# A decoder layer's expert stage: features on the partitions, weights as the stationary operand

## The chip, the core and the metric

The kernel runs on one core of a Trainium2 chip. The metric is device time in microseconds. A core has TensorE (PE, matmuls into PSUM), VectorE (DVE), ScalarE (ACT), GpSimd (POOL) and SyncE (SP); each runs its own list of instructions in order, and semaphores tie the lists together.

## The reference

A decoder layer on x of 4 x 256 tokens with 128 features: self attention with fixed-point rounding, cross attention to 1601 context rows, and a mixture of 8 experts of which each token uses 2. All is f32. The part that the change touches:

```
gout = x @ Wgate + bgate ; top 2 of 8, softmax over the two weights
x1 = x @ W1[e] + b1[e]                  # 128 -> 256
x2 = x @ W2[e] + b2[e]
z  = x1 * x2
g  = z @ Wg[e] + bg[e]                  # 256 -> 256
o  = silu(g) * (z @ Wl[e] + bl[e])
y  = o @ W3[e] + b3[e]                  # 256 -> 128
out = x + sum over the two chosen experts of weight * y
```

## The kernel before

The layer is one program: projections and self attention (to about 270 us), cross attention (to about 605 us), then layer norm, routing and the expert stage. Routing sorts the 2048 (token, expert) pairs into blocks of 128 rows that belong to one expert each: at most NBLK = 23 blocks. The rows go through HBM (`xdisp`): POOL scatters them there, SP loads one block after the other into a ring of 6 (`xblk`), and POOL scatters the results to `ydisp` from a ring of 3 (`yblk`). At the end the two results of each token are loaded and added. Which expert a block has is read from `table` into a register of each engine that needs it (`value_load`), and the weights of all experts lie in SBUF: `w12` (W1 and W2 side by side, 512 columns an expert), `wgl` (Wg and Wl, 2 x 512), `w3_sb`.

One block before, with tokens on the partitions between the layers. Line numbers are those of the profile:

- `block_T` (L1205, TensorE) transposes the block's rows, `block_move` (L1448, ScalarE) copies them to SBUF.
- `up` (L1217): the transposed tokens are the stationary operand, 512 weight columns stream past; result 128 tokens x 512.
- `zed_of` (VectorE): adds the bias (L1817) from `bias_bc`, a copy of all biases on each of the 128 partitions, and multiplies the two halves (L1818).
- `zed_transposes` (L1225) and `zed_move` (L1454): the product, turned, for the next layer.
- `gate_linear` (L1233): two matmuls of 512 columns, accumulated.
- `gl_bias` (L1823), `gate_silu` (L1460), `ogl_of` (L1830).
- `ogl_transposes` (L1243) and `ogl_move` (L1466), `down` (L1251), `y_move` (L1473, which also scales by the routing weight), the scatter (L815).

The blocks are interleaved by hand. In iteration j TensorE's list has: up(j), ogl_transposes(j-2), block_T(j+1), gate_linear(j-1), the register load for j+1, zed_transposes(j), down(j-2). VectorE's has zed_of(j), gl_bias(j-1), ogl_of(j-1), and after the first zed_of the table of the later blocks. ScalarE's has ogl_move(j-2), block_move(j+1), zed_move(j), gate_silu(j-1), y_move(j-2). PSUM homes and SBUF tiles of each step are doubled.

The experts' weights are loaded by POOL's queue during cross attention: Wg and Wl near 298 us, W1, W2, W3 and the four biases near 550 us, the biases as broadcasts to 128 partitions (1 MB each). SP's queue loads small rows (`nmT`, 3 KB, L597) that cross attention's score matmuls (L1054) wait for.

Of the kernel before, what the change touches and what calls it, by code (L numbers as in the profile page):

```python
# [9 lines left out]
ALU = mybir.AluOpType  # L10
# [176 lines left out]
def decoder_layer(nc, x, ctx_in, mask, w_qkv, w_proj, b_proj, wo_w, wo_b, Wgate, bgate,  # L187
                  W1, b1, W2, b2, Wg, bg, Wl, bl, W3, b3, out):
    stack = ExitStack()
    with stack:  # L190
# [85 lines left out]
        bias_bc = cut(region_b, NE * 4 * FF)  # L276
# [59 lines left out]
        zedT = cut(region_p, 2 * FF).rearrange("p (u f) -> p u f", u=2)  # L336
# [3 lines left out]
        oglT = cut(region_p, 2 * FF).rearrange("p (u f) -> p u f", u=2)  # L340
# [139 lines left out]
        zed_T = sem("zed_T")  # L480
        zedT_made = sem("zedT_made")
# [4 lines left out]
        ogl_T = sem("ogl_T")  # L486
        oglT_made = sem("oglT_made")
# [46 lines left out]
        zT_bank, xT_bank = pair[2][:, 0:256], pair[2][:, 512:640]  # L534
        oT_bank, y_bank = pair[3][:, 0:256], pair[3][:, 512:640]
# [84 lines left out]
        def _(pool):  # L620
# [141 lines left out]
            def experts_load():  # L762
# [9 lines left out]
                for n, v in enumerate((b1, b2, bg, bl)):  # L772
                    pool.dma_start(bias_bc.rearrange("p (e f) -> p e f", e=NE)[:, :, n * FF:(n + 1) * FF],
                                   v.partition_broadcast(128)).then_inc(experts_loaded, 16)
# [47 lines left out]
        def _(pe):  # L822
# [352 lines left out]

            finish_tiles(B - 1, 0, pair[2])
            finish_tiles(B - 1, 1, pair[3][:, 0:256])
            finish_tiles(B - 1, 2, pair[3][:, 256:512])
# [34 lines left out]
            def up(j):  # L1213

                pe.wait_ge(xblkT_made, j + 1)
                wait(pe, z_made, j - 1)
                pe.matmul(up_bank[j % 2], xblkT[:, j % 2, :], w12[:, bass.ds(expert[j] * (2 * FF), 2 * FF)],  # L1217
                          start=True, stop=True).then_inc(up_mm, 1)

            def zed_transposes(j):  # L1220

                pe.wait_ge(z_made, j + 1)
                wait(pe, zedT_made, j)
                for f in range(2):
                    last = pe.transpose(zT_bank[:, f * 128:(f + 1) * 128], zed[:, j % 2, f * 128:(f + 1) * 128], ident[:, :])  # L1225
                last.then_inc(zed_T, 1)

            def gate_linear(j):

                pe.wait_ge(zedT_made, j + 1)  # L1230
                wait(pe, glb_made, j - 1)
                for f in range(2):
                    last = pe.matmul(gl_bank[j % 2], zedT[:, j % 2, f * 128:(f + 1) * 128],  # L1233
# [26 lines left out]
            for j in range(NBLK + 2):  # L1260
                if j < NBLK:
                    up(j)
                if j >= 2:
                    ogl_transposes(j - 2)
# [6 lines left out]
                if j < NBLK:  # L1271
                    zed_transposes(j)
# [595 lines left out]
```

## Time and profile before

| | us |
|---|---|
| three runs, median (lowest to highest) | 750.12 (749.71 to 751.29) |
| the profiled execution | 743.64 |
| its span, first to last instruction | 741.9 |
| busy: PE, DVE, ACT, POOL | 585.1, 531.5, 445.2, 185.7 |
| mean granted TensorE clock | 0.906 of 2.4 GHz |

Durations below come from the one profiled execution. A busy share says how full an engine is, not whether it sets the time: for that the chain of waits is read. Names such as `region_p` stand for many tiles cut from one buffer, so lines tell steps apart. TensorE executes an f32 matmul as two passes, each with a weight load (`PEld`) of its own; in the timeline "x4" merges four passes, and the time given runs from the first's start to the last's end.

### The profile page before, as it was taken

To read this page: it belongs to the slowest core of one execution; us is meant where nothing else is said; L and a number is where in the kernel's file an instruction comes from. 1 tells how busy PE (TensorE), PEld (TensorE's weight loads), DVE (VectorE), ACT (ScalarE), POOL (GpSimd) and SP (SyncE) were. 2 spreads that over 40 slices of the span, in tenths; PEclk is the share of its full clock that TensorE was granted. 3 is DMA by queue.
4 is the path that set the end of the run, shared out by engine and by line. 5 is a ranking of instruction groups with operands and counts; after the bars stand their busy time and mean duration, and the time that the engine had idled before them with its cause. 6 is when DMAs were issued, how large, how long until landed. Compare 5 with 4: busy or idle time off the path is not lost.

```text
span 741.9 us, 13437 instructions
## 1 busy us (share of the span) xinstructions
PE 585.1 (79%) x4759; PEld 289.4 (39%) x4759; DVE 531.5 (72%) x896; ACT 445.2 (60%) x818; POOL 185.7 (25%) x234
## 2 busy tenths in 40 slices
PE   3775548888896856899999988889886875999981
PEld 2453335555554743333333333333331232444441
DVE  4466698899889987688888888788783245555541
ACT  3553338888889412687867876778674752334330
POOL 4325570000011233332115101500040044122222
PEclk9876679999999985999999999999996795999996
DMA  8332364724576802601090109000029001011103
GB/s 209 97 121 92 100 219 175 199 60 122 143 158 131 151 1 89 227 3 47 2 222 24 47 2 211 35 3 1 2 79 319 2 28 51 22 33 34 33 21 93
DMA packets 32667, 66.91 MB, mean 90 GB/s; under 512 B 4542, under 2 KB 21322, under 8 KB 32164
## 3 DMA queue, kind: packets, MB, share of 16 engines
q0 software_dynamic: 8960, 45.07, 22.9%
q1 hardware_dynamic: 22068, 20.31, 9.1%
q10 hardware_dynamic: 1584, 0.79, 0.4%
q8 instruction: 36, 0.59, 0.3%
q14 instruction: 19, 0.16, 0.1%
HBM read 46.45 MB, written 19.30 MB: 89 GB/s over the span
## 4 chain that ended last, share of the span: by engine, by line
PE 43%; DVE 32%; ACT 9%; issue 8%; DMA 5%; SPq 1%; DVEq 0%; ACTq 0%; POOLq 0%; POOL 0%
DVE smax L1647 12%; PE pair L1079 10%; DVE region_p L1550 6%; PE pair L1054 6%; PE pair L1233 5%; PE pair L1009 4%; PE pair L910 3%; PE pair L874 3%; DVE region_p L1520 3%; ACT region_p L1410 2%; ACT region_p L1329 2%; DVE region_p L1823 2%; PE pair L896 2%; DVE region_p L1553 2%; PE pair L963 1%
## 5 line engine op out<-in xcount | busy, mean ns | idle before, releaser
L1647 DVE TENSOR_REDUCE smax<-pair 128x2 f32<-128x1024 f32 x192 | 225.5, 1218 | 55.7 <-PE pair L1009 55.0
L1410 ACT ACTIVATE region_p<-pair 128x1024 f32<-128x1024 f32 (+3 forms) x277 | 217.5, 812 | 68.3 <-PE pair L1054 63.1
L910 PE MATMUL pair<-ident,region_p 128*128 128x128 f32 x256 | 39.3, 302 | 45.3 <-DVE region_p L1553 45.3
L1520 DVE SCALAR_TENSOR_TENSOR region_p<-region_p 128x1024 int16<-128x1024 int16 (+1 forms) x56 | 67.6, 1229 | 9.1 <-ACT region_p L1315 6.6
L1079 PE MATMUL pair<-region_p 128*32 128x256 f32 (+1 forms) x832 | 69.8, 410 | 0.5 <-ACT region_p L1417 0.4
L1079 PE MATMUL pair<-region_p,region_b 128*32 128x256 f32 (+1 forms) x832 | 66.5, 391 | 0.4 <-ACT region_p L1417 0.4
L1550 DVE TENSOR_SCALAR region_p<-region_p,rnorm 128x256 f32<-128x256 f32 x128 | 62.1, 548 | 1.1
L1054 PE MATMUL pair<-region_b,region_k 59*128 59x256 bf16 (+1 forms) x416 | 54.7, 273 | 8.2 <-ACT region_p L1410 4.0
L1009 PE MATMUL pair<-region_k,region_b 56*128 56x512 bf16 (+1 forms) x256 | 44.5, 365 | 16.8 <-DVE smax L1647 15.6
L910 PEld LDWEIGHTS pair<-ident,region_p 128*128 128x128 f32 x256 | 31.0, 154 | 59.9 <-DVE region_p L1553 59.2
L1329 ACT ACTIVATE region_p<-region_p 128x256 f32<-128x256 int16 x128 | 51.3, 409 | 0.0
L724 POOL CAST nparts<-nmax 128x8 bf16<-128x8 f32 x16 | 3.1, 191 | 184.5 <-DVE nmax L1657 184.5
L1233 PE MATMUL pair<-region_g,region_p 128*128 x92 | 44.7, 608 | 0.0
L1337 ACT ACTIVATE region_p<-pair 128x1024 f32<-128x1024 f32 x32 | 32.5, 1014 | 17.1 <-PE pair L910 17.1
L921 PE MATMUL pair<-region_p 128*64 128x256 f32 x256 | 36.4, 407 | 7.5 <-ACT region_p L1337 6.8
L815 POOL DMA_INDIRECT ydisp<-region_p x23 | 22.3, 970 | 76.7 <-ACT region_p L1473 76.7
L896 PE MATMUL pair<-region_p 64*128 64x256 f32 x256 | 39.3, 427 | 2.4 <-ACT region_p L1321 1.8
L1321 ACT ACTIVATE region_p<-pair 128x1024 int16<-128x1024 f32 x32 | 32.7, 1022 | 12.7 <-PE pair L896 12.4
L1054 PE MATMUL pair<-wpT,region_k 59*128 59x256 bf16 (+1 forms) x208 | 29.5, 298 | 11.9 <-DMA wpT<-nmT 7.1
L1054 PEld LDWEIGHTS pair<-region_b,region_k 59*128 59x128 bf16 (+1 forms) x416 | 22.4, 96 | 37.5 <-issue 17.0
L874 PE MATMUL pair<-xnT,wT 128*128 128x512 f32 x64 | 35.2, 680 | 0.6 <-ACT wT L1309 0.6
L666 POOL DMA_DIRECT2D region_b<-in_mask_Bx1xSxS_ff x8 | 4.7, 583 | 117.1 <-ACT region_b L1342 95.9
(244 smaller groups left out, 968.3 us busy)
## 6 DMA issues: line engine op xcount, KB each, us to landing
kimg<-region_k SPq DMA_DIRECT2D x56, 200.1 KB
region_k<-kimg POOLq DMA_DIRECT2D x8, 1400.9 KB, 12.4
region_b<-in_mask_Bx1xSxS_ff POOLq DMA_DIRECT2D x12, 800.5 KB, 7.0
region_p<-in_mask_Bx1xSxS_ff POOLq DMA_DIRECT2D x4, 800.5 KB, 13.2
region_b<-in_ctx SPq DMA_DIRECT2D x4, 768.0 KB
region_k<-in_L_ffn_W POOLq DMA_DIRECT2D x3, 1024.0 KB, 8.4
xdisp<-region_x POOLq DMA_DIRECT2D x1, 2322.0 KB, 21.1
xdisp<-region_x POOLq DMA_DIRECT2D x1, 2257.5 KB, 18.4
```

The lines of the kernel that those rows point to most:

```text
L874: last = pe.matmul(qkv_home(hp, c)[:, n * 512:(n + 1) * 512], wT[:, c * 128:(c + 1) * 128], xnT[:, n * 512:(n + 1) * 512], start=True, sto ...
L896: last = pe.matmul(pair[0][:, h * 512 + t * 256:h * 512 + (t + 1) * 256], qf[rows, b * S + t * 128:b * S + (t + 1) * 128], kf[rows, b * S: ...
L910: last = pe.transpose(pair[1][:, c:c + 128], attn[:, b % 2, a:a + 128], ident[:, :])
L1009: last = pe.matmul(out_, qstack[b][64 * a:64 * a + KROWS, 2 * g + j, q * 128:(q + 1) * 128], kstack[64 * a:64 * a + KROWS, b % 2, 2 * g + ...
L1054: last = pe.matmul(st_bank[n % 3][0:rows, j * 256:(j + 1) * 256], kstack[64 * a:64 * a + SROWS, b % 2, 2 * g + j, keys], qstack[b][64 * a: ...
L1079: last = pe.matmul(pair[3][32 * h:32 * h + 32, 512 + s % 2 * S:512 + (s % 2 + 1) * S], v_heads[b % 2][0:rows, t, c:c + 32], pT[0:rows, n / ...
L1233: last = pe.matmul(gl_bank[j % 2], zedT[:, j % 2, f * 128:(f + 1) * 128], wgl[:, bass.ds(expert[j] * (4 * FF) + f * 2 * FF, 2 * FF)], star ...
L1329: last = act.activation(expd[:, b % 2, k * 256:(k + 1) * 256], dotf[:, b % 2, k * 256:(k + 1) * 256], ACT.Exp, scale=1.0 / FXP, accum_out= ...
L1410: act.activation(pT[0:rows, first // 3 % 2, k:k + size], home[0:rows, 0:size], ACT.Exp).then_inc(expt_made, 1)
L1520: return dve.scalar_tensor_tensor(out_, floor16, 0.0, floor16, ALU.is_lt, ALU.add)
L1550: last = dve.tensor_scalar(attn_h[:, b % 2, k * 256:(k + 1) * 256], expd[:, b % 2, k * 256:(k + 1) * 256], rnorm[:, k:k + 1], -0.5, ALU.mu ...
L1647: last = dve.tensor_reduce(units[:, :, c // 3, c % 3], both, AX.X, ALU.max)
```

## The change

The expert stage keeps features on the partitions from the first layer to the last. In `up` and `gate_linear` the weights are now the stationary operand, cut in pieces of 128 columns, and the 128 tokens stream: 4 and 8 matmuls of 128 columns instead of 1 and 2 of 512. Their result has features on the partitions, as the next layer's input needs it, so both pairs of transposes and their moves to SBUF are gone; `down` takes `ogl` as the stationary operand and gives tokens on the partitions again. ScalarE copies each block's weights to a fixed place first, into `staged` (two slots): `stage_up` 128x512 and `stage_gl` 128x1024, from the address that its own register of the expert gives. The biases become one value a partition, broadcast along the tokens: they are loaded once as 32 rows (8 KB a DMA instead of 1 MB), transposed by TensorE (`biases_T`, between the pieces of cross attention's finish) and moved by ScalarE.

```diff
-        bias_bc = cut(region_b, NE * 4 * FF)
+        bias_nat = cut(region_b, FF)
+        bias_T = cut(region_b, 8 * NE)
...
-        zedT = cut(region_p, 2 * FF).rearrange("p (u f) -> p u f", u=2)
-        oglT = cut(region_p, 2 * FF).rearrange("p (u f) -> p u f", u=2)
+        staged = cut(region_p, 2 * 6 * FF).rearrange("p (u f) -> p u f", u=2)
...
-                    pool.dma_start(bias_bc.rearrange("p (e f) -> p e f", e=NE)[:, :, n * FF:(n + 1) * FF],
-                                   v.partition_broadcast(128)).then_inc(experts_loaded, 16)
+                    pool.dma_start(bias_nat[n * NE:(n + 1) * NE, :], v).then_inc(experts_loaded, 16)
...
+            def biases_T():
+
+                pe.wait_ge(experts_loaded, 16 * 9)
+                for f in range(2):
+                    last = pe.transpose(bias_bank[:, f * 4 * NE:(f + 1) * 4 * NE], bias_nat[0:4 * NE, f * 128:(f + 1) * 128],
+                                        ident[0:4 * NE, 0:4 * NE])
+                last.then_inc(bias_rows_T, 1)
+
             finish_tiles(B - 1, 0, pair[2])
             finish_tiles(B - 1, 1, pair[3][:, 0:256])
+            biases_T()
             finish_tiles(B - 1, 2, pair[3][:, 256:512])
...
             def up(j):
 
                 pe.wait_ge(xblkT_made, j + 1)
+                pe.wait_ge(wup_staged, j + 1)
                 wait(pe, z_made, j - 1)
-                pe.matmul(up_bank[j % 2], xblkT[:, j % 2, :], w12[:, bass.ds(expert[j] * (2 * FF), 2 * FF)],
-                          start=True, stop=True).then_inc(up_mm, 1)
-
-            def zed_transposes(j):
-
+                for m in range(4):
+                    last = pe.matmul(up_bank[j % 2][:, m * 128:(m + 1) * 128],
+                                     staged[:, j % 2, m * 128:(m + 1) * 128],
+                                     xblkT[:, j % 2, :], start=True, stop=True)
+                last.then_inc(up_mm, 1)
+
+            def gate_linear(j):
+
+                pe.wait_ge(wgl_staged, j + 1)
                 pe.wait_ge(z_made, j + 1)
-                wait(pe, zedT_made, j)
-                for f in range(2):
-                    last = pe.transpose(zT_bank[:, f * 128:(f + 1) * 128], zed[:, j % 2, f * 128:(f + 1) * 128], ident[:, :])
-                last.then_inc(zed_T, 1)
-
-            def gate_linear(j):
-
-                pe.wait_ge(zedT_made, j + 1)
                 wait(pe, glb_made, j - 1)
-                for f in range(2):
-                    last = pe.matmul(gl_bank[j % 2], zedT[:, j % 2, f * 128:(f + 1) * 128],
-                                     wgl[:, bass.ds(expert[j] * (4 * FF) + f * 2 * FF, 2 * FF)],
-                                     start=(f == 0), stop=(f == 1))
+                for m in range(4):
+                    for f in range(2):
+                        last = pe.matmul(gl_bank[j % 2][:, m * 128:(m + 1) * 128],
+                                         staged[:, j % 2, (f + 1) * 2 * FF + m * 128:(f + 1) * 2 * FF + (m + 1) * 128],
+                                         zed[:, j % 2, f * 128:(f + 1) * 128], start=(f == 0), stop=(f == 1))
                 last.then_inc(gl_mm, 1)
 
-            def ogl_transposes(j):
+            def down(j):
 
                 pe.wait_ge(ogl_made, j + 1)
-                wait(pe, oglT_made, j)
-                for f in range(2):
-                    last = pe.transpose(oT_bank[:, f * 128:(f + 1) * 128], ogl[:, j % 2, f * 128:(f + 1) * 128], ident[:, :])
-                last.then_inc(ogl_T, 1)
-
-            def down(j):
-
-                pe.wait_ge(oglT_made, j + 1)
                 wait(pe, yblk_made, j)
                 for f in range(2):
-                    last = pe.matmul(y_bank, oglT[:, j % 2, f * 128:(f + 1) * 128],
+                    last = pe.matmul(y_bank, ogl[:, j % 2, f * 128:(f + 1) * 128],
                                      w3_sb[:, bass.ds(expert[j] * (2 * D) + f * D, D)],
                                      start=(f == 0), stop=(f == 1))
                 last.then_inc(y_mm, 1)
...
             for j in range(NBLK + 2):
                 if j < NBLK:
                     up(j)
-                if j >= 2:
-                    ogl_transposes(j - 2)
                 if j + 1 < NBLK:
                     block_T(j + 1)
                 if 1 <= j <= NBLK:
                     gate_linear(j - 1)
                 if j + 1 < NBLK:
                     expert_of(j + 1)
-                if j < NBLK:
-                    zed_transposes(j)
                 if j >= 2:
                     down(j - 2)
                 if j == NBLK:
...
+            act.wait_ge(bias_rows_T, 1)
+            act.activation(bias_T.rearrange("p (e n f) -> p e n f", e=NE, n=4),
+                           bias_bank.rearrange("p (f n e) -> p e n f", f=2, n=4), ACT.Copy).then_inc(biasT_made, 1)
...
-            def zed_move(j):
-
-                act.wait_ge(zed_T, j + 1)
-                wait(act, gl_mm, j - 1)
-                act.activation(zedT[:, j % 2, :], zT_bank, ACT.Copy).then_inc(zedT_made, 1)
...
-            def ogl_move(j):
-
-                act.wait_ge(ogl_T, j + 1)
-                wait(act, y_mm, j - 1)
-                act.activation(oglT[:, j % 2, :], oT_bank, ACT.Copy).then_inc(oglT_made, 1)
...
+            def stage_up(j):
+
+                if j in (0, AHEAD):
+                    act.wait_ge(table_made, 1 + j // AHEAD)
+                expert[j] = act.value_load(table[0:1, 1, j:j + 1], min_val=0, max_val=NE - 1)
+                wait(act, up_mm, j - 1)
+                act.activation(staged[:, j % 2, 0:2 * FF], w12[:, bass.ds(expert[j] * (2 * FF), 2 * FF)],
+                               ACT.Copy).then_inc(wup_staged, 1)
+
+            def stage_gl(j):
+
+                wait(act, gl_mm, j - 1)
+                act.activation(staged[:, j % 2, 2 * FF:6 * FF], wgl[:, bass.ds(expert[j] * (4 * FF), 4 * FF)],
+                               ACT.Copy).then_inc(wgl_staged, 1)
+
+            act.wait_ge(experts_loaded, 16 * 9)
+            expert = [None] * NBLK
+            stage_up(0)
             block_move(0)
+            stage_gl(0)
             for j in range(NBLK + 2):
-                if j >= 2:
-                    ogl_move(j - 2)
                 if j + 1 < NBLK:
                     block_move(j + 1)
-                if j < NBLK:
-                    zed_move(j)
+                    stage_up(j + 1)
+                if j >= 2:
+                    y_move(j - 2)
                 if 1 <= j <= NBLK:
                     gate_silu(j - 1)
-                if j >= 2:
-                    y_move(j - 2)
+                if j + 1 < NBLK:
+                    stage_gl(j + 1)
             act.wait_ge(comb_T, 1)
...
-            dve.wait_ge(experts_loaded, 16 * 9)
+            dve.wait_ge(biasT_made, 1)
...
-                wait(dve, zed_T, j - 1)
-                chain.step(dve.tensor_tensor(upb, up_bank[j % 2], bias_bc[:, bass.ds(expert[j] * (4 * FF), 2 * FF)], ALU.add))
+                wait(dve, gl_mm, j - 1)
+                chain.step(dve.tensor_tensor(upb.rearrange("p (m t) -> p m t", m=4), up_bank[j % 2].rearrange("p (m t) -> p m t", m=4),
+                                             bias_T[:, bass.ds(expert[j] * 8, 4)].unsqueeze(2).broadcast_to([128, 4, 128]), ALU.add))
                 dve.tensor_tensor(zed[:, j % 2, :], upb[:, 0:FF], upb[:, FF:2 * FF], ALU.mult).then_inc(z_made, 1)
 
             def gl_bias(j):
 
                 dve.wait_ge(gl_mm, j + 1)
-                dve.tensor_tensor(glb[:, j % 2, :], gl_bank[j % 2], bias_bc[:, bass.ds(expert[j] * (4 * FF) + 2 * FF, 2 * FF)],
+                dve.tensor_tensor(glb[:, j % 2, :].rearrange("p (m t) -> p m t", m=4), gl_bank[j % 2].rearrange("p (m t) -> p m t", m=4),
+                                  bias_T[:, bass.ds(expert[j] * 8 + 4, 4)].unsqueeze(2).broadcast_to([128, 4, 128]),
                                   ALU.add).then_inc(glb_made, 1)
...
-                wait(dve, ogl_T, j - 1)
+                wait(dve, y_mm, j - 1)
```

TensorE's list for one block in the regular part, before. Names are PSUM pair and the SBUF regions: pair0 is up, pair1 gate and linear, pair2 the block's and the product's transposes, pair3 the other transposes and down; an ISA row sets an address from a register. From up(j) to the first transpose of the next product (the second and down(j-2) follow):

```order
L1217 ISA [waits z_made,xblkT_made]
L1217 MATMUL pair0<-region_k,region_p 128x512
L1243 MATMUL pair3<-ident,region_p 128x128 [waits oglT_made,ogl_made]
L1243 MATMUL pair3<-ident,region_p 128x128
L1205 MATMUL pair2<-ident,region_p 128x128 [waits xblkT_made,xblk_loaded_1]
L1233 ISA [waits glb_made,zedT_made]
L1233 MATMUL pair1<-region_g,region_p 128x512
L1233 ISA
L1233 MATMUL pair1<-region_g,region_p 128x512
L1211 TENSOR_LOAD table
L1211 ISA x2
L1225 MATMUL pair2<-ident,region_p 128x128 [waits zedT_made,z_made]
```

The list after, from up(j) to the end of down(j-2):

```order
L1227 MATMUL pair0<-region_p 128x128 [waits z_made,wup_staged,xblkT_made]
L1227 MATMUL pair0<-region_p 128x128 x3
L1213 MATMUL pair2<-ident,region_p 128x128 [waits xblkT_made,xblk_loaded_0]
L1239 MATMUL pair1<-region_p 128x128 [waits glb_made,z_made,wgl_staged]
L1239 MATMUL pair1<-region_p 128x128 x7
L1219 TENSOR_LOAD table
L1219 ISA x2
L1249 ISA [waits yblk_made,ogl_made]
L1249 MATMUL pair3<-region_k,region_p 128x128
L1249 ISA
L1249 MATMUL pair3<-region_k,region_p 128x128
```

The four transposes with `ident` and their waits (`zedT_made`, `oglT_made`) are gone, matmuls of 512 columns stand as four or eight of 128, and the waits for `wup_staged` and `wgl_staged` are new. The register load stays between gate and down.

ScalarE's list for one block before, beginning with the move of the turned product (pair3):

```order
L1466 ACTIVATE region_p<-pair3 128x256 [waits y_mm,ogl_T]
L1448 ACTIVATE region_p<-pair2 128x128 [waits up_mm,xblk_T]
L1454 ACTIVATE region_p<-pair2 128x256 [waits gl_mm,zed_T]
L1460 ACTIVATE region_p<-region_p 128x256 [waits ogl_made,glb_made]
L1473 ACTIVATE region_p<-pair3,region_p 128x128 [waits ydisp_written_1,y_mm]
```

And after, beginning with the token move (pair2):

```order
L1445 ACTIVATE region_p<-pair2 128x128 [waits up_mm,xblk_T]
L1465 TENSOR_LOAD table
L1465 ISA x2
L1467 ISA [waits up_mm]
L1467 ACTIVATE region_p<-region_k 128x512
L1458 ACTIVATE region_p<-pair3,region_p 128x128 [waits ydisp_written_0,y_mm]
L1451 ACTIVATE region_p<-region_p 128x256 [waits ogl_made,glb_made]
L1473 ISA [waits gl_mm]
L1473 ACTIVATE region_p<-region_g 128x1024
```

The two moves of 128x256 are gone; a register load and a 128x512 copy stand behind the token move, and a 128x1024 copy stands last, behind the silu.

## Rows read from the trace of the kernel before

**Rows 1.** Stretches: us, busy us (instructions) per engine, clock, DMA share, GB/s.
```profile
core 0: us, PE busy (x) PEld busy (x) DVE busy (x) ACT busy (x) POOL busy (x), PEclk, DMA share, GB/s
622.00:631.00 9.00, 7.16 (x13) 2.71 (x12) 5.71 (x25) 1.22 (x4) 4.06 (x4) 0.60 0.19 54
...
660.00:680.00 20.00, 18.62 (x74) 9.63 (x73) 11.17 (x20) 8.04 (x25) 4.85 (x5) 1.00 0.11 31
```

**Rows 2.** Chain of waits: start us, us, what ran.
```profile
639.47 0.70 DVE region_p L1823
...
664.25 0.70 DVE region_p L1823
664.97 0.42 ACT region_p L1460
665.42 0.44 DVE region_p L1830
665.90 0.44 PE pair L1243 x2
666.45 1.80 PE pair L1233 x4
...
721.67 0.70 DVE region_p L1823
```

**Rows 3.** Timeline of one block: start, us, engine, line, idle before.
```profile
664.16 0.61 PE L1251 MATMUL pair<-region_k,region_p 128*128 x4
...
664.60 1.02 PE L1217 MATMUL pair<-region_k,region_p 128*128 x2
...
666.18 0.27 PE L1205 MATMUL pair<-ident,region_p 128*128 128x128 f32 x1
666.25 0.69 DVE L1817 TENSOR_TENSOR region_p<-pair,region_b 128x512 f32<-128x512 f32 x1 [0.40 <-issue]
...
666.29 1.95 PE L1233 MATMUL pair<-region_g,region_p 128*128 x4
...
666.98 0.42 DVE L1818 TENSOR_TENSOR region_p<-region_p 128x256 f32<-128x256 f32 x1
```

**Rows 4.** Timeline of the output projection; then a group of weight loads.
```profile
246.74 3.82 PE L963 MATMUL pair<-wpT,region_g 128*128 128x128 f32 x32
...
L1251 PEld LDWEIGHTS pair<-region_k,region_p 128*128 128x128 f32 x56 | 7.4, 192 | 0.0
```

**Rows 5.** Groups by form, ScalarE: busy us, mean ns, idle before.
```profile
L1448 ACT ACTIVATE region_p<-pair 128x128 f32<-128x128 f32 x15 | 4.1, 272 | 0.0
...
L1473 ACT ACTIVATE region_p<-pair,region_p 128x128 f32<-128x128 f32 x15 | 5.3, 350 | 0.0
...
L1342 ACT ACTIVATE region_b<-region_b 128x1601 f32<-128x1601 f32 x8 | 12.3, 1533 | 0.0
```

**Rows 6.** Timeline and chain, start and end of the expert blocks.
```profile
628.55 2.21 PE L1233 MATMUL pair<-region_g,region_p 128*128 x4
...
630.07 0.69 DVE L1817 TENSOR_TENSOR region_p<-pair,region_b 128x512 f32<-128x512 f32 x1 [0.58 <-issue]
...
633.34 1.88 PE L1233 MATMUL pair<-region_g,region_p 128*128 x4
...
719.61 1.91 PE L1233 MATMUL pair<-region_g,region_p 128*128 x4
...
723.80 0.39 ACT region_p L1466
```

**Rows 7.** DMA issues, 545 to 585 us (KB, us to landing); a stretch; a timeline row.
```profile
region_k<-in_L_ffn_W POOLq DMA_DIRECT2D x3, 1024.0 KB, 8.4
...
region_b<-in_L_ffn_bl POOLq DMA_DIRECT2D x1, 1024.0 KB, 20.2
...
555.00:560.00 5.00, 0.52 (x8) 0.04 (x6) 1.20 (x2) 0.59 (x1) 1.43 (x2) 0.75 1.03 335
...
562.45 0.61 PE L1054 MATMUL pair<-wpT,region_k 59*65 59x256 bf16 x4 [6.92 <-DMA wpT<-nmT]
```

More of the change, by code:

```diff
@@ L479, in decoder_layer @@
         z_made = sem("z_made")
-        zed_T = sem("zed_T")
-        zedT_made = sem("zedT_made")
         gl_mm = sem("gl_mm")
@@ L485, in decoder_layer @@
         ogl_made = sem("ogl_made")
-        ogl_T = sem("ogl_T")
-        oglT_made = sem("oglT_made")
+        bias_rows_T = sem("bias_rows_T")
+        biasT_made = sem("biasT_made")
+        wup_staged = sem("wup_staged")
+        wgl_staged = sem("wgl_staged")
         y_mm = sem("y_mm")
@@ L533, in decoder_layer @@
         gl_bank = (pair[1][:, 0:512], pair[1][:, 512:1024])
-        zT_bank, xT_bank = pair[2][:, 0:256], pair[2][:, 512:640]
-        oT_bank, y_bank = pair[3][:, 0:256], pair[3][:, 512:640]
+        xT_bank, y_bank = pair[2][:, 512:640], pair[3][:, 512:640]
+        bias_bank = pair[0][:, 800:800 + 8 * NE]
         rank_bank, total_bank = pair[1][:, 512:512 + NT * NE], (pair[0][:, 768:768 + NE], pair[3][:, 512:512 + NE])
```

## The prediction

> **What bounds the kernel now.** I read the table of stretches first. From 622 us on, the profile shows the expert stage, 23 blocks of 128 token rows. From 660 to 680 us TensorE is busy 93% of the time, VectorE 56%, ScalarE 40%, and the granted clock is 1.00 (2.4 GHz); from 622 to 631 us it is 0.60, so part of the start runs at 1.2 GHz [rows 1]. Busy time doesn't say which engine decides, so I read the chain of waits next. One block runs: VectorE adds the gate bias (L1823), ScalarE takes the silu (L1460), VectorE multiplies (L1830), TensorE transposes the product (L1243), and only behind that stands TensorE's next gate and linear matmul (L1233), which releases the next L1823. The first row of L1823 in that regular part is at 639.47 and the last at 721.67, 20 periods apart: 82.20 / 20 = 4.11 us a block [rows 2]. So for 1.56 us of a block (0.70 + 0.42 + 0.44) TensorE's next big matmul is held by other engines. TensorE fills much of that time with other blocks' work, but its order has the transpose of block j-2 ahead of the gate matmul of block j-1, and so the loop closes.
>
> **What the change removes and adds on TensorE.** An f32 matmul with 128 weight columns shows as two passes. From the timeline of one block: the down projection is 4 passes of 128 columns in 0.61 us, of which a lone end is 0.27, so (0.61 - 0.27) / 3 = 0.113 us a pass; the gate matmul is 4 passes of 512 columns in 1.95, (1.95 - 0.59) / 3 = 0.45, its first pass a little late; up is 2 passes in 1.02, 0.43 apart [rows 3]. Before, one block streams 6 x 0.43 + 4 x 0.113 + 5 transposes x 0.11 = 3.58 us. After, the weights are stationary and the 128 tokens stream: up is 4 matmuls = 8 passes, gate and linear 8 matmuls = 16 passes, down is unchanged at 4, and four of the five transposes are gone: 28 x 0.113 + 0.11 = 3.27 us. Columns streamed are the same; only the transposes go (0.3 us), but weight loads per block rise from 15 to 29. Is a weight load behind each 128 columns hidden? The output projection L963 is just that: 32 passes with 32 different weight loads in 3.82 us, (3.82 - 0.27) / 31 = 0.115 us, though one load takes 0.192 us by itself [rows 4]. So 0.113 to 0.115 a pass, 3.27 to 3.33 a block; I take 3.27, since the first passes of L963 were the late ones.
>
> **What it removes from the loop.** With features on the partitions the product feeds the down matmul as it is; the gate matmul of block j-1 now stands behind up(j) and one transpose, and the latest thing of another block that it waits for is the gate bias add of block j-3. The old loop (0.70 + 0.42 + 0.44 + transposes + 1.80) is open. What is late next?
>
> VectorE's loop: bias add, wait for silu, product, register load, next up-bias, product, next bias add. By the rows L1823 starts at 664.25, L1817 at 666.25 (with 0.40 of idle for the register load), L1818 at 666.98 and takes 0.42: 3.15 us, if it never waited for TensorE [rows 2, 3]. The new operands are f32 of the same sizes, one of them broadcast; I keep 0.69. So VectorE comes at 3.15, under TensorE's 3.27.
>
> ScalarE's loop: it loses two moves (L1454, L1466) and gets two copies, 128x512 and 128x1024, from SBUF to SBUF. The trace has no such copy; the nearest are silu, 256 elements in 0.416, and L1342, 1601 elements in 1.533, both from SBUF: 0.83 ns an element, so 0.63 and 1.05 us [rows 2, 5]. Per block 0.27 + 0.63 + 0.35 + 0.42 + 1.05 = 2.72 us, less than 3.27. But the order matters: the copy for gate and linear stands behind silu(j-1), and behind it stand the token move and the up copy that up(j+2) waits for. From the end of gate matmul j-1 on the array: 0.3 until VectorE starts, 0.72 bias, 0.42 silu, 1.05, 0.27, 0.63, 0.05 = 3.44 us. TensorE has in that time down 0.45, up 0.90, transpose 0.11, gate 1.81, down 0.45 = 3.72 us of its own. Slack 0.28 us. So the copies are off the path by a little, and each 0.1 us over my estimate beyond that costs 0.05 a block (the loop spans two blocks). The register load on ScalarE runs while the 1.05 us copy ahead of it is still executing.
>
> TensorE's own register load (one a block) stands between the gate matmul and down. Before, no gap is seen after it, because 0.43 us passes were queued ahead. Now 16 short passes are. If they are issued faster than they execute, nothing shows; if not, up to the 0.40 that VectorE shows is added per block. Bounds 3.27 to 3.67; I take 3.27: as many columns stand in front of it as before, and the 16 weight loads with them.
>
> **The sum.** Regular part: before, from the gate matmul of block 1 (633.34) to that of block 22 (719.61), 86.3 us [rows 6]. After: 20 periods of 3.27 and a last one without up and transpose, 1.81 + 0.45 = 2.26: 67.7. Saved 18.6. Start: in both, VectorE is busy with the block table until about 630 and starts L1817 of block 1 at 630.07, so the product of block 1 is there at 631.2. After, TensorE has gate(0) (from 628.55, to about 630.7 with the clock rising on the way), up(2) and a transpose ahead, so gate(1) starts near 631.7 and not at 633.34, where it waited for a transpose, a move and the product of block 0: saved 1.6. The first staging copies stand ahead of up(0) on ScalarE and cost about 0.1 to 0.3; I take 1.5 in all, bounds 0 to 1.6. End: one transpose pair and one move drop out behind the last product, 0.44 + 0.39 + 0.14 to 0.18 of hand-over: 1.0 [rows 2, 6]. The bias transposes fall into the last block of cross attention's finish, where TensorE waits for VectorE anyway: 0.
>
> The biases. Before, four broadcasts of 1 MB each stand behind 3 MB of weights on POOL's queue, and a matmul of cross attention waits 6.92 us for 3 KB that SP's queue loads at the same time [rows 7]. After, the four are 8 KB each. At the 335 GB/s of that stretch the weights alone take 3.1 MB / 0.335 MB per us = 9 us from about 551 on, so to about 560 or 562, which is when those 3 KB came (the matmul starts at 562.45). I take 0, bounds 0 to 2 us of gain; the half clock (1.2 GHz) behind that stall may also end otherwise.
>
> Sum: 18.6 + 1.5 + 1.0 = 21.1 us. Against the profiled execution, 743.64 us (span 741.9): 722.5. The runs' median was 6.5 us over the profiled execution; the change touches nothing in what makes that up, so I take the same 21.1 from 750.12: 729.0 us.
>
> **A rule that speaks against it.** L963 gives 0.115 us a pass with a new weight load in each. The Trainium skill, "TensorE: Matmul & The Clock Gate", Part 3, under "The mechanism", says that weight loads overlap running matmuls only where the row group differs; here all use all rows. With its figure of 107 ns for 128 weight columns (section on LDWEIGHTS) in series with a stream of 107 ns, an estimate is 28 x 0.213 = 6.0 us a block, some 40 us slower than before. The trace disagrees in L963. The same page's Part 2 has the next weights loading in the background while a matmul runs; with that the trace agrees.
>
> **Rivals.** (a) TensorE's issue or its register load shows: up to 0.40 a block, 20 x 0.40 = 8 us: 737. For it: VectorE's 0.40. Against: no gap behind L1233 now. (b) ScalarE's loop decides: the copies are dearer than their SBUF neighbours, say by half (0.84 us more, less the slack 0.28, over two blocks = 0.28 a block, 5.6 us): 735. For it: slack of only 0.28. Against: all ScalarE rows lie on one line per element. (c) Slower: the array waits for each weight load. It decides from 4.11 us a block, (4.11 - 0.11) / 28 = 0.143 us a pass; with the whole 0.192 in series behind 0.113 a block takes 8.6 us and the kernel about 840. Against: L963. (d) The broadcasts' going frees the 3 KB load: 2 us more gain and 1 to 2 of half clock: 725.
>
> **How the numbers follow.** Forecast (TensorE streams without gaps, 729) 0.70; (a) 0.12; (b) 0.07; (c) 0.03; (d) 0.06; 0.02 that some wait I don't see takes all of it. A change below 0.2%, 1.5 us, can't be told from none here. Faster 0.95, same 0.02, slower 0.03. The range goes from (d), 725, to just short of (a), 736.
>
> **What would show it.** Right: L1823's successor starts every 3.2 to 3.35 us, TensorE's rows in the expert stage follow each other with no idle time, the new ScalarE copies read 0.63 and 1.05 us, VectorE's bias adds 0.69 with a wait of about 0.1 ahead. Wrong: idle time ahead of the up matmuls put down to ScalarE (b), ahead of down without a releaser (a), passes more than 0.12 us apart (c), or the expert stage shorter by another amount than 21 us while the part before 600 us moved (d).

## The result, and the profile after

| | before | after |
|---|---|---|
| median of 4 runs each, us (lowest to highest) | 750.7 (749.71 to 751.67) | 725.95 (725.03 to 728.25) |
| ratio, 95% interval | | 0.9675 (0.9648 to 0.9702) |
| profiled execution / its span, us | 743.64 / 741.9 | 725.64 / 723.9 |
| TensorE's mean clock | 0.906 | 0.914 |

The change saves 3.3%; the forecast was 729.0 (725 to 736). The span shrank by 18.0 us. Where it went is read by stretches first. Kernel after, a stretch of the start of the expert stage and one of its regular part:

```profile
core 0: us, PE busy (x) PEld busy (x) DVE busy (x) ACT busy (x) POOL busy (x), PEclk, DMA share, GB/s
631.00:634.00 3.00, 3.00 (x17) 3.00 (x16) 2.19 (x9) 0.91 (x2) 0.20 (x1) 0.54 0.07 22
...
660.00:680.00 20.00, 20.00 (x181) 20.00 (x181) 13.73 (x26) 14.60 (x30) 6.04 (x6) 1.00 0.17 45
```

TensorE went from 18.62 of 20 us to 20.00 [rows 1], and its weight loads are busy all the time too. The chain of waits of the kernel after (start us, us, what ran) no longer leaves TensorE, where before it went through VectorE and ScalarE [rows 2]:

```profile
660.65 0.89 PE pair L1227 x8
661.54 0.11 PE pair L1213
661.65 1.79 PE pair L1239 x16
663.44 0.45 PE pair L1249 x4
663.88 0.89 PE pair L1227 x8
...
667.12 0.89 PE pair L1227 x8
```

Up is L1227, the token transpose L1213, gate and linear L1239, down L1249. Two blocks from 660.65 to 667.12: 3.235 us a block, for 4.11. The timeline of one block of the kernel after, beside [rows 3]:

```profile
661.08 0.42 ACT L1451 ACTIVATE region_p<-region_p 128x256 f32<-128x256 f32 x1
...
661.40 1.04 ACT L1473 ACTIVATE region_p<-region_g 128x1024 f32 x1
661.49 1.95 PE L1239 MATMUL pair<-region_p 128*128 128x128 f32 x16
661.53 0.42 DVE L1835 TENSOR_TENSOR region_p<-region_p 128x256 f32<-128x256 f32 x1 [0.48 <-ACT region_p L1451]
...
662.37 0.69 DVE L1820 TENSOR_TENSOR region_p<-pair,region_b 128x512 f32<-128x512 f32 x1 [0.41 <-issue]
662.51 0.62 ACT L1467 ACTIVATE region_p<-region_k 128x512 f32 x1
```

VectorE waits for silu and for its register load, not for TensorE; it keeps its results ahead of need. Groups by form of the kernel after (busy us, mean ns, idle before) give the copies' price, beside [rows 5]:

```profile
L1473 ACT ACTIVATE region_p<-region_g 128x1024 f32 x23 | 23.9, 1041 | 0.0
L1467 ACT ACTIVATE region_p<-region_k 128x512 f32 x23 | 14.3, 620 | 0.8 <-issue 0.8
```

Start and end of the expert stage in the kernel after, beside [rows 6]:

```profile
624.86 0.47 PE L1213 MATMUL pair<-ident,region_p 128*128 128x128 f32 x1 [0.30 <-issue]
...
629.46 2.04 PE L1227 MATMUL pair<-region_p 128*128 128x128 f32 x8 [1.48 <-ACT region_p L1467]
...
631.51 3.03 PE L1239 MATMUL pair<-region_p 128*128 128x128 f32 x16
...
635.38 1.95 PE L1239 MATMUL pair<-region_p 128*128 128x128 f32 x16
...
702.46 2.02 PE L1239 MATMUL pair<-region_p 128*128 128x128 f32 x16
```

and the first row of the stage in the kernel before:

```profile
621.81 0.46 PE L1205 MATMUL pair<-ident,region_p 128*128 128x128 f32 x1 [0.31 <-issue]
```

From the gate matmul of block 1 to that of block 22: 86.3 us before, 67.1 after, 19.2 saved. From the first transpose to the gate matmul of block 1: 11.5 and 10.5, 1.0 saved. From the last gate matmul to the end of the span: 22.3 and 21.4, 0.9 saved. So the stage, from its first transpose to the end of the span, takes 120.1 us before and 99.0 after: 21.1 saved. Yet the span shrank by 18.0 only, since in this pair of executions the stage began 3.05 us later. That is not the change's doing, as the second profile of the kernel before shows below.

The time up to the stage moves by several us from one profile to the next: its first transpose starts between 621.81 and 630.50 us in the 14 profiles, and between 623.90 and 630.50 in the kernels that have the code of the kernel after up to there. So the experiments are read by the stage's own length (span less the start of its first transpose) and by the period of a block in the chain; the medians stand beside. Each ratio is to runs of the kernel before on the same chip, whose medians were 750.7, 749.9, 749.8, 747.3 and 748.1 us in the five sets of runs, so ratios and not medians are compared across sets.

| kernel | median, us (runs) | ratio to before | stage, us | period, us |
|---|---|---|---|---|
| before | 750.7 (4) | | 120.1 | 4.11 |
| before_again | 747.16 (1) | | 120.0 | |
| after | 725.95 (4) | 0.9675 | 99.0 | 3.235 |
| after_again | 726.17 (4) | 0.9695 (0.9653 to 0.9736) | 99.05 | |
| wide_biases | 727.75 (6) | 0.9718 (0.9680 to 0.9757) | 99.2 | |
| no_copies | 725.0 (6) | 0.9681 (0.9648 to 0.9714) | 98.1 | |
| copies_twice | 742.09 (4) | 0.9884 (0.9836 to 0.9933) | 110.8 | 3.755 |
| down_twice | 737.15 (4) | 0.9816 (0.9767 to 0.9865) | 108.9 | 3.685 |
| down_half | 724.0 (6) | 0.9663 (0.9629 to 0.9696) | 96.7 | 3.08 |
| before_late_T | 736.13 (4) | 0.9854 (0.9822 to 0.9885) | 109.2 | 3.60 |
| before_down_twice | 749.03 (10) | 1.0014 (0.9990 to 1.0038) | 120.9 | 4.115 |
| warm | 730.06 (6) | 0.9729 (0.9685 to 0.9772) | 98.7 | |
| warm_late | 726.8 (6) | 0.9723 (0.9686 to 0.9759) | 98.5 | |
| early_up | 727.45 (6) | 0.9717 (0.9674 to 0.9760) | 98.5 | |

### The profile page after: what moved, and what is told of

Read it like the earlier page. It is cut to its first block, busy times and chain, and to the rows that moved or that the text cites. A ratio compares the mean times of both kernels' runs of the same rounds, so it can differ in the third digit from the quotient of the medians.

```text
span 723.9 us, 14051 instructions
## 1 busy us (share of the span) xinstructions
PE 570.0 (79%) x5083; PEld 319.3 (44%) x5083; DVE 529.5 (73%) x896; ACT 464.3 (64%) x819; POOL 184.7 (26%) x234
## 4 chain that ended last, share of the span: by engine, by line
PE 48%; DVE 28%; ACT 8%; issue 8%; DMA 5%; SPq 1%; ACTq 0%; POOLq 0%; DVEq 0%; POOL 0%
DVE smax L1650 12%; PE pair L1078 10%; PE pair L1053 6%; DVE region_p L1553 6%; PE pair L1239 6%; PE pair L1008 4%; PE pair L909 4%; PE pair L1227 3%; PE pair L873 3%; DVE region_p L1523 3%; ACT region_p L1404 2%; ACT region_p L1323 2%; PE pair L895 2%; DVE region_p L1556 2%; PE pair L962 2%
## 5 line engine op out<-in xcount | busy, mean ns | idle before, releaser
L1523 DVE SCALAR_TENSOR_TENSOR region_p<-region_p 128x1024 int16<-128x1024 int16 (+1 forms) x56 | 67.2, 1222 | 10.9 <-ACT region_p L1309 8.5
L1239 PE MATMUL pair<-region_p 128*128 128x128 f32 x368 | 46.0, 279 | 0.0
L1239 PEld LDWEIGHTS pair<-region_p 128*128 128x128 f32 x368 | 44.1, 196 | 0.0
L1053 PEld LDWEIGHTS pair<-region_b,region_k 59*128 59x128 bf16 (+1 forms) x416 | 22.4, 96 | 37.8 <-issue 15.8
```

The lines of the kernel that those rows point to most:

```text
L1053: last = pe.matmul(st_bank[n % 3][0:rows, j * 256:(j + 1) * 256], kstack[64 * a:64 * a + SROWS, b % 2, 2 * g + j, keys], qstack[b][64 * a: ...
L1239: last = pe.matmul(gl_bank[j % 2][:, m * 128:(m + 1) * 128], staged[:, j % 2, (f + 1) * 2 * FF + m * 128:(f + 1) * 2 * FF + (m + 1) * 128] ...
L1523: return dve.scalar_tensor_tensor(out_, floor16, 0.0, floor16, ALU.is_lt, ALU.add)
```

## The experiments

**Both kernels again** (before_again, after_again).

> The kernel before, unchanged, for a second profile: the first profiled execution (743.64 us) lies 6.5 us under the median of the runs. If the difference is in cross attention's stalls and half-clock stretches, the expert stage is the same 633.3 to 725.5 us long (92 us from gate matmul 1 to the last y_move) and the part before it is about 6 us longer. If it is in the expert stage, that is longer.

> The changed kernel, unchanged, for a second profile. In the first, TensorE's semaphores of the last cross-attention matmuls (600 to 610 us) came up to 5 us after the matmuls' own ends, and the stage before the experts ended 2.9 us later than before. If that is a chance of one execution, it is gone or elsewhere here and the span is about the same or up to 3 us shorter; if the change causes it, it stands at the same instructions.

Measured: spans 745.4 and 723.8, 21.6 us apart. In the second profile of before the stage starts at 625.38 instead of 621.81 and lasts 120.0 us. What differs sits at the end of cross attention. ScalarE's last move of it, first in before, then in before_again, then in after:

```profile
605.12 0.39 ACT L1417 ACTIVATE region_p<-pair 128x256 f32<-128x256 f32 x1 [0.76 <-PE pair L1079]
```
```profile
608.98 0.39 ACT L1417 ACTIVATE region_p<-pair 128x256 f32<-128x256 f32 x1 [6.28 <-remote]
```
```profile
603.28 0.64 PE L1078 MATMUL pair<-region_p 65*32 65x256 f32 x8 [0.60 <-issue]
609.47 0.39 ACT L1411 ACTIVATE region_p<-pair 128x256 f32<-128x256 f32 x1 [6.24 <-remote]
```

In the last two it has been idle for over 6 us; in after it starts 5.5 us (609.47 - 603.92) behind the modelled end of the matmul that it waits for. after_again has it at the same instruction (6.23 us), as would be so if the change caused it, but the unchanged kernel has it too, so it isn't the change; the first profile of before was an execution without it.

**The broadcasts** (wide_biases): the kernel after, with the four 1 MB broadcasts of before issued behind the weights and read by nobody.

```diff
+        wide = cut(region_b, NE * 4 * FF)
...
+                for n, v in enumerate((b1, b2, bg, bl)):
+                    pool.dma_start(wide.rearrange("p (e f) -> p e f", e=NE)[:, :, n * FF:(n + 1) * FF],
+                                   v.partition_broadcast(128)).then_inc(wide_loaded, 16)
```

> The changed kernel, but the four 1 MB broadcasts of the biases are loaded too, to a place that nobody reads, ahead of the small loads. My forecast: the same time as the changed kernel, within 1 us, since the stall for the 3 KB load ends with the 3 MB of weights either way. Rival (d): 2 to 4 us slower than the changed kernel, the stall being longer and the clock half for longer.

Measured: stage 99.2 us, ratio 0.9718 beside 0.9695, the median 1.6 us higher: more than the 1 us of the forecast and less than the 2 of the rival, with intervals that overlap. The wait for the 3 KB is [rows 7] 6.92 us before, and after, then in wide_biases:

```profile
560.98 0.61 PE L1053 MATMUL pair<-wpT,region_k 59*65 59x256 bf16 x4 [6.20 <-DMA wpT<-nmT]
```
```profile
563.10 0.61 PE L1059 MATMUL pair<-wpT,region_k 59*65 59x256 bf16 x4 [6.68 <-DMA wpT<-nmT]
```

Over all profiles it is 6.27 to 6.92 us in the five with the broadcasts (before_late_T has the 6.27) and 6.16 to 6.67 in the nine without (down_twice, early_up). The two groups overlap, so a shorter wait isn't shown, and it is at most some 0.7 us. The stall stays without the broadcasts. In the kernel after it ends as the DMA share falls, from 0.97 in 560 to 561 us to 0.13 in 561 to 563, which points to the 3 MB of weights; no run leaves these out.

**ScalarE's copies, taken away and doubled** (no_copies, copies_twice). In no_copies TensorE reads the weights of the first two layers in place.

```diff
-                act.activation(staged[:, j % 2, 0:2 * FF], w12[:, bass.ds(expert[j] * (2 * FF), 2 * FF)],
-                               ACT.Copy).then_inc(wup_staged, 1)
...
-                                     staged[:, j % 2, m * 128:(m + 1) * 128],
+                                     w12[:, m * 128:(m + 1) * 128],
```

> The changed kernel with ScalarE's two copies a block left out: TensorE takes the stationary weights in place, from expert 0 for every block (the choice of the expert is left out in the first two layers). TensorE theory: a period of 3.23 us stays, only the start is up to 1 us shorter: 725 to 726. ScalarE rival (b): the copies are on the path in places, 3 us or more gained.

copies_twice adds a second copy of the same size in front of each:

```diff
+                wait(act, spare_made, 2 * j)
+                act.activation(spare[:, 0:2 * FF], w12[:, bass.ds(expert[j] * (2 * FF), 2 * FF)],
+                               ACT.Copy).then_inc(spare_made, 1)
```

> The changed kernel with each of ScalarE's two weight copies of a block done twice, the first time into memory that nobody reads: +1.65 us of ScalarE work a block. By my theory TensorE's 3.235 us a block sets the pace of the changed kernel and ScalarE has only some 0.2 to 0.3 us of slack a block, measured through its loop with VectorE (two blocks of ScalarE's loop were 3.44 us beside the 3.72 it could have taken). The loop would then take over at 3.65 to 3.85 us a block: +9 to +13 us on 22 periods against the changed kernel. If ScalarE's copies lay in time that nobody waits for (slack over 1.65 us a block), 0 to +1 us. If ScalarE already set the pace (the rival in which its loop decides), the whole 1.65 us a block would show, +30 us or more.

Measured: without copies the stage is 1.0 us shorter, all of it in the start, where the second block's up layer waits 0.37 us instead of 1.48; in the regular part nothing goes (67.2 us for 67.1), so there the copies are free. Doubled, the stage is 11.8 us longer, in the range of the forecast (9 to 13), the block 3.755 us. Stretch of copies_twice, columns as above:

```profile
660.00:680.00 20.00, 18.34 (x154) 17.56 (x155) 11.80 (x22) 19.92 (x39) 4.86 (x5) 1.00 0.13 36
```

ScalarE is busy 19.92 of 20 us there: its work itself sets the pace, not a loop of waits. In the kernel after it has 14.60 of 20, 2.36 us a block of 3.235. The added copies cost 1.47 us a block, since successive ones start 0.52 and 0.95 us apart, less than their 0.62 and 1.04; 2.36 + 1.47 = 3.83 against 3.755 measured. The slack is therefore about 0.87 us a block in ScalarE's work; the 0.28 us of the forecast, over a loop of waits, was not separately tested, and the time came into the expected range by another way than the loop that was expected to take over. The ratios say 14 us (0.0189 x 750), somewhat more; in the profiles copies_twice begins its stage 5.75 us later than after_again. The added copies aren't the cause: the matmul behind the wait for the 3 KB already starts 5.4 us later (565.37 for 559.96), and no_copies begins its stage at 630.44. What the cause is stays open.

**TensorE's work, more and less** (down_twice, down_half), on the kernel after:

```diff
-                for f in range(2):
+                for f in (0, 1, 0, 1):
```
```diff
-                for f in range(2):
+                for f in range(1):
...
-                                     start=(f == 0), stop=(f == 1))
+                                     start=(f == 0), stop=True)
```

> The changed kernel with the down layer's two matmuls issued twice, the same result being written again: four more fp32 passes of 128 columns a block, 4 x 0.1116 = 0.446 us of TensorE. If TensorE's streaming sets the pace, as the forecast has it, 22 blocks x 0.446 = +9.8 us against the changed kernel (726 to 736), and the period is 3.68 us. If the loop through VectorE or ScalarE's work sets it, under +2 us.

> The changed kernel with only the first half of the down layer's product (it leaves out the features 128 to 255 of the hidden layer there): two passes fewer a block, TensorE 3.235 - 0.223 = 3.01 us. If TensorE alone sets the pace, -0.223 x 22 = -4.9 us against the changed kernel. If VectorE's loop of two blocks, which the forecast puts at 3.15 us a block, stands right behind it, the gain stops there: -1.9 us, and TensorE is idle for some 0.14 us of every block. If TensorE sets nothing, 0.

Measured for down_twice: +0.45 us a block, stage +9.9 us, and +9.1 us by the ratios (0.0121 x 750). Its chain:

```profile
660.24 0.89 PE pair L1227 x8
...
663.03 0.89 PE pair L1249 x8
663.92 0.89 PE pair L1227 x8
```

All of the added work shows: TensorE sets the pace. down_half takes 0.223 us of it away and gains 0.155 (3.08 us a block), and its stage is 2.3 us shorter, between the two numbers expected (1.9 and 4.9). It isn't 22 x 0.155 = 3.4, since in the kernel after too VectorE catches up at 3.07 to 3.11 us a block for six blocks, behind the table of the later blocks and in the middle of the stage. The timeline of down_half shows what stops the gain:

```profile
666.99 0.69 DVE L1820 TENSOR_TENSOR region_p<-pair,region_b 128x512 f32<-128x512 f32 x1 [0.40 <-issue]
...
667.71 0.42 DVE L1822 TENSOR_TENSOR region_p<-region_p 128x256 f32<-128x256 f32 x1
...
668.05 0.68 DVE L1827 TENSOR_TENSOR region_p<-pair,region_b 128x512 f32<-128x512 f32 x1
...
669.22 0.43 DVE L1835 TENSOR_TENSOR region_p<-region_p 128x256 f32<-128x256 f32 x1 [0.48 <-ACT region_p L1451]
...
670.07 0.69 DVE L1820 TENSOR_TENSOR region_p<-pair,region_b 128x512 f32<-128x512 f32 x1 [0.42 <-issue]
```

VectorE comes round in 3.08 us and nowhere in these rows waits for TensorE: the loop that the forecast put at 3.15. It stands 0.16 us behind TensorE in the kernel after.

**The same questions put to the kernel before** (before_late_T, before_down_twice). before_late_T only opens the loop: the transposes of a product stand between the two halves of the next block's gate matmul, and ScalarE's moves of the product and of the next tokens change places.

```diff
             def gate_linear(j):
...
                                     start=(f == 0), stop=(f == 1))
+                    if f == 0 and j >= 1:
+                        ogl_transposes(j - 1)
...
-                if j >= 2:
-                    ogl_transposes(j - 2)
                 if j + 1 < NBLK:
                     block_T(j + 1)
```

> The kernel before with one thing of the change alone: the gate matmul no longer stands behind the transposes of the product. On TensorE the two transposes of block j-2's product move from ahead of the gate and linear matmul of block j-1 to between its two halves; on ScalarE the move of that product changes places with the move of the next tokens. Orientation, copies, biases and all four transposes a block stay. By my reading the kernel before waited in a loop (gate matmul, bias, silu, product, transposes, next gate matmul) at 4.11 us a block with 3.58 us of TensorE work in it. If so, the block now takes 3.6 to 3.75 us and 8 to 11 us go of the some 21 that the whole change brings: 739 to 742 for 750. If the loop wasn't what set the pace, 0, and the whole gain of the change would be the shorter TensorE work, which can't be, since only 0.34 us a block of it go (0.34 x 22 = 7.5 us).

> The kernel before with the down layer's two matmuls issued twice, the same 4 x 0.1116 = 0.446 us of TensorE a block that cost the changed kernel 0.45 us a block. If the loop set the pace before, TensorE has 0.53 us a block to spare, and the added passes lie in its wait for the product's transposes: period 4.11 to 4.2, 0 to +2 us. If TensorE's streaming set it, +9.8 us.

Measured: before_late_T has a median 11.2 us below that of the runs of before beside it (747.33), and a stage shorter by 10.9 us (120.1 to 109.2), at the upper end of the 8 to 11 expected. Its chain:

```profile
660.70 0.86 PE pair L1217 x2
...
661.67 0.86 PE pair L1233 x2
662.53 0.22 PE pair L1245 x2
662.75 0.86 PE pair L1233 x2
...
663.83 0.46 PE pair L1253 x4
664.28 0.86 PE pair L1217 x2
...
671.51 0.87 PE pair L1217 x2
```

Three blocks in 10.81 us, 3.60 a block, all on TensorE: the 3.58 us of work that the forecast counted. The work of down_twice, 0.45 us a block in the kernel after, costs nothing there in the kernel before (4.115 us a block; the stage is 0.8 us longer, the ratio 1.0014): it falls into the wait of the loop. Chain of before_down_twice:

```profile
659.63 0.86 PE pair L1217 x2
660.50 0.27 PE pair L1243 x2
...
662.85 0.89 PE pair L1251 x8
663.75 0.86 PE pair L1217 x2
```

So the change does two things of about equal worth: it opens the loop (4.11 to 3.60, 10.9 us of the stage), and it shortens TensorE's work (3.60 to 3.235; with the shorter start and end the remaining 10.2 us, taken by subtraction). The first could have been had by an order alone.

**The half clock in the start, and one copy earlier** (warm, warm_late, early_up). TensorE's clock is at 1.2 GHz up to 633.8 us in the kernel after, 8.9 us into the stage. warm puts idle matmuls into TensorE's waits, warm_late only the last of these bursts and the one before it.

```diff
             finish_tiles(B - 1, 0, pair[2])
+            burst(pair[0][:, 0:512], 4)
             finish_tiles(B - 1, 1, pair[3][:, 0:256])
...
             gates(1)
+            burst(pair[0][:, 0:512], 4)
             ranks(1)
...
+                if j == 0:
+                    burst(pair[2][:, 0:512], 4)
```

> The changed kernel with 19 matmuls of 512 columns on identities put into TensorE's waits between the end of cross-attention and the second expert block (4 before the transposes of the context, 1 before its output product, 6 before the transposes of the norm, 4 before the ranks, 4 behind the second block's transpose); nobody reads what they write. In the changed kernel's trace the granted clock is at half from 606.5 to 633.8 us, in which TensorE has some 11 us of matmuls on the path, first of all 2.08 + 2.04 us of the up layers of two blocks and 3.03 us of a gate layer that take 0.89 and 1.79 later. If its being idle there is what keeps the clock low, the clock comes back earlier and 2 to 5 us go: 721 to 724. If it doesn't, or the added matmuls themselves delay the path by as much, 0 to +2 us.

> The changed kernel with only 8 of the 19 idle matmuls of the kernel 'warm': 4 ahead of the ranks, 4 behind the transpose of the second expert block. In the trace of 'warm' the clock was up again 5.0 us behind the first block's transpose (633.7 for 628.67) and in the changed kernel's 8.9 us behind it (633.8 for 624.86), but the third gate layer then waited 0.67 us for VectorE, and the matmuls put ahead of the context's transposes and the output product brought 1.2 us of wait. If that is the whole account, this one keeps the gain in the start of the expert stage without the loss: 0.8 to 1.5 us less than the changed kernel, near what can be measured. If the added matmuls delay the ranks, 0 to +1.

```diff
             stage_up(0)
             block_move(0)
             stage_gl(0)
+            stage_up(1)
```

> The changed kernel with one copy earlier: ScalarE copies the first-layer weights of block 1 before it moves block 1's tokens, in a time in which it is idle (from 626.6 to 628.0 us in the changed kernel), so that the up layer of block 1 waits for the move alone. In the changed kernel's trace that layer waits 1.48 us for the copy, and without copies (the kernel 'no_copies') 0.37. By my reading 1.0 to 1.1 us go from the start of the expert stage and nothing else moves: 725 for 726, just under what can be measured, and the stage from the first block's transpose to the end lasts 98.0 instead of 99.0 us. If VectorE's table of the later blocks holds the gate layer of block 1 instead, as in the kernel 'warm', less than 0.5 us go.

Measured: none can be told from the kernel after (0.9729, 0.9723 and 0.9717, whose intervals all hold after_again's 0.9695). The mechanisms work: in warm the clock is back at 2.4 GHz in pieces (columns as above), and falls again in between:

```profile
617.00:620.00 3.00, 0.97 (x5) 0.49 (x5) 0.39 (x1) 0.33 (x2) 0.53 (x1) 1.00 0.07 22
620.00:624.00 4.00, 3.59 (x10) 1.71 (x10) 2.18 (x10) 1.39 (x2) 0.00 (x0) 0.57 0.23 53
624.00:627.00 3.00, 1.93 (x10) 0.96 (x10) 1.28 (x11) 1.97 (x4) 0.40 (x1) 0.98 0.20 46
627.00:631.00 4.00, 2.53 (x24) 2.19 (x25) 2.17 (x16) 3.13 (x5) 0.91 (x1) 0.50 0.00 0
```

and in early_up the second up layer waits 0.37 us instead of 1.48, as expected. But in all three the gate layer of block 1 then waits for VectorE, which has the table of the later blocks to make first; early_up's rows:

```profile
630.78 2.07 PE L1227 MATMUL pair<-region_p 128*128 128x128 f32 x8 [0.37 <-ACT region_p L1445]
...
636.81 2.02 PE L1239 MATMUL pair<-region_p 128*128 128x128 f32 x16 [0.71 <-DVE region_p L1824]
```

So 0.3 to 0.6 us of the stage go (98.7, 98.5 and 98.5 for 99.05) instead of 1.0 to 5, and no version here is shown to beat the kernel after. In warm the way from the context's transposes to the stage is also 0.8 us longer.

## Why the prediction was right

- **The loop was the bound before**: shown, by before_late_T (its opening alone gives half the gain) and before_down_twice (more TensorE work is free).
- **TensorE at 3.27 a block**: 3.235. A pass with a new 128-column weight load takes 1.79 / 16 = 0.112 us, beside 0.113 in the sum and 0.115 in L963 [rows 4]. The regular part saved 19.2 for 18.6 us.
- **Weight loads are hidden** (rival c, decides from 0.143 us a pass): they are, in all passes; PEld is busy 20.00 of 20 us and TensorE waits nowhere. The rule of the Trainium skill, "TensorE: Matmul & The Clock Gate", Part 3, "The mechanism", that loads overlap only where the row group differs does not hold for these f32 passes, which all use all rows: by the estimate from it a block would have taken 6.0 us.
- **The register load on TensorE shows nothing** (rival a): L1249 follows L1239 without a gap. VectorE's 0.40 stays.
- **Copies 0.63 and 1.05 us** (rival b): 0.620 and 1.041. ScalarE decides nothing in the regular part; no_copies gains nothing there.
- **VectorE's loop 3.15**: 3.08, seen in down_half.
- **Start 1.5 us**: 1.0. The clock came back later in the stage than the step took it to. Stretch of the kernel before:

```profile
628.00:634.00 6.00, 5.13 (x15) 2.20 (x14) 3.79 (x12) 1.52 (x5) 0.21 (x1) 0.90 0.08 22
```

  A clock of 0.90 over 6 us is 1.2 us at half, so up to 629.2, 7.4 us behind the first transpose; the 0.54 of 631 to 634 in the kernel after is 2.8 us at half, up to 633.8, 8.9 us behind it. The gate matmul of block 0 starts as far behind the first transpose as before (6.65 and 6.74 us), but its row reads 3.03 us where the step took 2.15. The step's price for the first copies, 0.1 to 0.3 us, was too low as well: without them (no_copies) the gate matmul of block 1 starts 9.5 us behind the first transpose, for 10.5 in the kernel after, and the clock is back 6.2 us behind it. So they cost 1.0 us, the later clock included.
- **End 1.0**: 0.9.
- **Biases 0, bounds 0 to 2** (rival d): the stall stays without the broadcasts, and no shorter wait can be told from the spread of the profiles. That the 3 MB of weights are its cause is argued from the DMA share, not shown by a run.
- **The sum**: 21.1 forecast, 21.1 measured within the stage, and 21.6 between the spans of the second pair of profiles. That the first two agree to 0.1 us is luck: the regular part gave 0.6 more and start and end 0.6 less than forecast.
- **From the profile to the median** the step was weak. It took 722.5 for the profiled execution and 6.5 us more for the median. Measured: 725.64, with a median 0.3 above. The first profile of before was a short execution (743.64 beside 747.16 of the second, and runs from 744.66 to 752.62), so its 6.5 us were its own, and not something that the kernel carries into the other. The forecast for the median missed by 3.05 us. Of the medians' difference, 24.75 us (22.4 to 26.4 by the interval), 21.1 are located; the ratio of the second set of runs, 0.9695 (0.9653 to 0.9736), has 21.1 us (0.972) in its interval, and the first has not. Whether 2 to 3 us more go somewhere ahead of the stage stays open; no run here singles them out.

## What to carry to other kernels

Read the wait that closes the loop before counting work: TensorE at 93% busy here had 0.53 us a block to spare, and adding 0.45 us was free, while after the change the same addition cost all of it. A change of layout that removes a step from such a loop brings its work and its wait; try first whether another order brings the wait alone. When an edit has made one engine the bound, ask at what distance the next one stands: here VectorE follows at 0.16 us a block, and down_half's saving on TensorE stopped there. And compare stages within the profile rather than spans, where an unrelated stretch moves by 3 us and more from one execution to the next.

## What was not expected of the hardware

- An engine can start well behind the modelled end of the matmul that it waits for. At the end of cross attention ScalarE starts 5.5 us behind it in most profiles, 4.1 in early_up and 0.1 in before. In warm it happens to VectorE as well, 2.1 us behind the modelled end at 617.49:

```profile
619.61 0.43 DVE L1691 COPY region_p<-pair 128x256 f32<-128x256 f32 x1 [2.68 <-remote]
```

  Whether the signal is late or the modelled end too early, and why, is open.
- ScalarE's instructions overlap a little: a copy of 1.04 us is followed by the next 0.95 us after its start, so 23 copies' durations overstate what they occupy by about a tenth.
- The clock can rise and fall within a few us: 1.00 from 617 to 620, 0.57 from 620 to 624, 0.98 from 624 to 627 and 0.50 from 627 to 631 in warm.
